# Second layer's attention: weighing by the values two key tiles in a row, and a quad's output copied out one step later

## Chip, cores and metric

One NeuronCore of one Trainium2 chip runs the whole program. The metric is the device time of one execution in microseconds. The five engines run their own instruction streams and meet at semaphores: TensorE (PE; PEld is its weight load), VectorE (DVE), ScalarE (ACT), GpSimd (POOL) and SyncE (SP), which here issues the DMAs.

## What is computed

A model of two layers over `x` (4 x 256 tokens of width 256), each layer with a cross attention to a context of 1601 keys per batch and a feed-forward part. The change touches only the second layer's attention:

```python
q = _qdq(x) @ _qdq(wq).T + bq
k, v = jnp.split(cond @ wkv.T + bkv, 2, axis=-1)
# 16 heads of 16, 256 queries, 1601 keys, 4 batches
attn = jax.nn.softmax(jnp.einsum('bnhd,bmhd->bhnm', q, k) * scale, axis=-1)
o = jnp.einsum('bhnm,bmhd->bnhd', attn, v).reshape(B, N, C)
out = _qdq(o) @ _qdq(wp).T + bp
```

After it come the residual and the second layer's feed-forward part (up, gate, down, expert).

## The kernel before

The second layer's attention is the last half of the program. It is cut into 16 quads: a quad is four heads of one batch, four quads to a batch. A quad takes 13 steps, one for each tile of 128 keys (the last has 65), named here by quad and step: q3.11 is step 11 of quad 3. A step consists of these parts:

- **Scores** (L1053): four matmuls of 256 columns, keys times queries of four heads, into PSUM banks 2 and 3 for even steps, 4 and 5 for odd ones. The operands carry three extra rows that subtract each query's maximum.
- **Exponential** (L1444): one ACTIVATE of 128x1024 on ScalarE, from those banks into one of three buffers `pr`. It waits for the scores (`sc_mm`) and for the weighing of three steps earlier (`av_mm`), which has read the buffer.
- **Weighing** (`weigh`, L1074): for each of the four heads, a matmul of 17 columns of stationary values against 256 moving columns, in float32. The trace shows it as two passes for each head, so eight matmuls. The four heads write to partitions 0, 32, 64 and 96 of bank 6, so they are in four column groups of the array and start within some 10 ns of each other. A step weighs the exponentials of the step before it. Bank 6 gathers a quad's 13 steps; then ScalarE copies it out (`out_copy`, L1431, which waits for the quad's 13th weighing), and only then may the next quad's first weighing start (`po_rdy`).
- **Maxima** (L963 on TensorE, L1633 on VectorE): the scores of the next quad are computed once more, in 32 chunks of 128 queries by 400 keys, and VectorE takes each chunk's maximum. The chunks alternate between banks 0 and 1, so TensorE may be at most two chunks ahead: chunk n waits until chunk n-2 has been reduced. At the end of the 32, VectorE makes the shift rows out of them in a chain of small operations (L1636 to L1644), TensorE turns them (`shift`, L1035, step 11) and ScalarE copies them into the queries; the next quad's scores wait for that.
- **Other work** beside it by a table (`BESIDE`): keys (L851, "k") and values (L861, "v") of the next batches, turning the output (L1083, "out", step 2 of the next quad), and the rest of the layer of the batch before. Its banks are all bank 7, taken in turns.

`schedule()` decides how many maxima chunks stand in which step (mostly two or three). Inside a step `pace` spreads them over the step's PE columns: a chunk is issued whenever the share of columns passed is ahead of the share of chunks issued.

The keys of half a batch need a long way before their maxima can start: keys on TensorE, bias on ScalarE, three splitting operations of the POOL (L628, L630, L632), three DMAs out to `kscr` and six DMAs back into the stacked layout `kst` (L545). The DMAs back overwrite a stack in use, so they also wait for the scores of two stages (a stage is two quads) earlier. `max_scores` for the first chunk of a stage waits for them (`k_stk`).

Of the kernel before, what the change touches and what calls it, by code (L numbers as in the profile page):

```python
# [28 lines left out]
B, LQ, D = 4, 256, 256  # L29
# [18 lines left out]
KT = (KEYS + P - 1) // P  # L48
# [3 lines left out]
QUADS = STAGES * 2  # L52
STEPS = QUADS * KT
# [58 lines left out]
def kind(job):  # L112

    return job[-1] if job[0] == "tail" else job[0]
# [7 lines left out]
def step_work(jobs):  # L122

    cost = {"k": 8 * 401, "v": 16 * D, "out": 2 * 4 * P, "shift": 8 * P, "up": 16 * D, "down": 16 * D,
            "expert": 16 * D, "turn_x": 4 * 4 * P, "turn_o": 4 * P, "project": 4 * D, "gate": 4 * 4 * E}
    return 4 * LQ + 4 * LQ + sum(cost.get(kind(j), 0) for j in jobs)
# [10 lines left out]
def first_chunks(t, third):  # L137

    slot = 3 * (t - TILES) + third
    return range(slot * NMAX // 6, (slot + 1) * NMAX // 6)  # L140


BESIDE = schedule()


def program(nc, x_in, ctx_in, ctx0_in, seg_in, ident_in, tabs_in, kk_in, ones_in, wkvc_in, wkr_in, wkrs_in,
# [3 lines left out]
    with ExitStack() as ctx:  # L150
# [8 lines left out]
        def bank(i, n=1):  # L159
            return ps[:, i * 512:(i + n) * 512]  # L160
# [524 lines left out]
        def _(pe):  # L685
# [169 lines left out]
            def values(b, j, bnk, between=None):  # L855
                for i in range(2 * j, min(2 * j + 2, KT)):
                    n = P if i < KT - 1 else KLAST
                    for k in range(FC):
                        if i % 2 + k >= 1 and between:
                            between(4 * D)  # L860
                        last = mm(bank(bnk)[0:n, (i % 2) * D:(i % 2 + 1) * D], ctxT[:, k, i * P:i * P + n],  # L861
                                  wkvT[:, k, D:2 * D], start=k == 0, stop=k == FC - 1)
                last.then_inc(v_mm, 1)
# [87 lines left out]
            def max_scores(quad, n):  # L951

                b, s, u, c = quad // 4, quad // 2, n // len(CH), n % len(CH)
                h = 4 * (quad % 4) + u // 2
                ca = 8 * len(CH) * quad + n
                if n == 0:
                    pe.wait_ge(k_stk[s % 2], 96 * (s // 2 + 1))
                    pe.wait_ge(q_stk[b], 96)
                if ca >= 2:
                    pe.wait_ge(mx_rdy, ca - 1)  # L960
                a, m = CH[c]
                q0 = b * LQ + (u % 2) * P
                mm(bank(ca % 2)[:, 0:m], qst[0:SROWS, h, q0:q0 + P], kst[0:SROWS, s % 2, h % HALF, a:a + m],  # L963
                   start=True, stop=True).then_inc(mx_mm, 1)
# [218 lines left out]
            shift(0)  # L1183
            pe.wait_ge(v_ev, NV + 5)
            values(1, 6, 4)
            for quad in range(QUADS + 2):
                for kt in range(KT):
                    jobs = BESIDE.get((quad, kt), [])
                    maxima = [j for j in jobs if j[0] == "max"]
                    others = [j for j in jobs if j[0] != "max"]  # L1190

                    total, count = step_work(others), len(maxima)
                    passed = [0]

                    def pace(columns):

                        passed[0] += columns
                        while maxima and (count - len(maxima)) * total < count * passed[0]:
                            max_scores(*maxima.pop(0)[1:])

                    if quad < QUADS:
                        pace(1)
                        scores(quad, kt, 0)
                        pace(2 * LQ)
                        scores(quad, kt, 2)
                        pace(2 * LQ)
                        if quad or kt:
                            weigh(KT * quad + kt - 1)
                        pace(4 * LQ)
                    elif quad == QUADS and kt == 0:  # L1210
                        weigh(STEPS - 1)
                    beside(others, pace)
                    while maxima:
                        max_scores(*maxima.pop(0)[1:])


        @block.scalar
        def _(act):
# [208 lines left out]
            def out_copy(quad):  # L1427
                act.wait_ge(av_mm, KT * (quad + 1))
                if quad >= 2:
                    act.wait_ge(ot_mm, quad - 1)  # L1430
                fn(poS[quad % 2], bank(6)[:, 0:LQ], ACT.Copy).then_inc(po_rdy, 1)  # L1431
# [4 lines left out]
            for quad in range(QUADS + 2):  # L1436
                for kt in range(KT):
                    if quad < QUADS:
                        i = KT * quad + kt
                        n = P if kt < KT - 1 else KLAST  # L1440
                        act.wait_ge(sc_mm, i + 1)
                        if i >= 3:
                            act.wait_ge(av_mm, i - 2)
                        fn(pr[i % 3][0:n, :], bank(2 + 2 * (i % 2), 2)[0:n, :], ACT.Exp, scale=SCALE1)\  # L1444
                            .then_inc(ex_rdy, 1)
                    if kt == 0 and 1 <= quad <= QUADS:
                        out_copy(quad - 1)
                    beside(quad, kt)

# [438 lines left out]
```

## Time and profile before

| what | value |
|---|---|
| median of 3 runs | 852.65 us (852.61 to 862.78) |
| span of the profiled execution | 856.0 us |
| TensorE busy | 774.2 us, 90% |
| VectorE busy | 579.5 us, 68% |
| ScalarE busy | 383.9 us, 45% |
| GpSimd busy | 187.4 us, 22% |
| first exponential of the second attention | 374.9 us |
| last exponential | 831.6 us |

The attention's 208 steps take the stretch from 374.9 to 832 us. TensorE's matmuls are pipelined, so "busy" counts a matmul of 256 columns as some 270 ns although the next one starts 110 ns later. Where a price is wanted, the starts of successive groups are to be compared, not the durations. A bracket at a row's end gives the idle time of the engine before that row and who ended it.

### The profile page before, as it was taken

The numbers are of one execution on the slowest core, as the hardware profiler recorded it, in microseconds if no ns is written. First come the engines' busy times: TensorE is split into PE (matmuls) and PEld (weight loads), VectorE is DVE, ScalarE is ACT, GpSimd is POOL, SyncE is SP. The second block draws the span as 40 slices with busy tenths as digits, with TensorE's granted clock in tenths as the row PEclk, the third lists the DMA queues.
The fourth block names the chain that finished last, engine by engine and source line by source line (L and its number), as shares of the span: only waits on it lengthen the run. The fifth ranks groups of instructions, "written<-read, shape, count | busy, mean of one in ns | idle before, by whom it ended". The sixth has DMA issues, their size and how long they took to land.

```text
span 856.0 us, 12968 instructions
## 1 busy us (share of the span) xinstructions
PE 774.2 (90%) x5027; PEld 434.2 (51%) x5027; DVE 579.5 (68%) x1290; ACT 383.9 (45%) x563; POOL 187.4 (22%) x136
## 2 busy tenths in 40 slices
PE   6998999977999898889989899989899989889996
PEld 3534777744665565644434455534445544335434
DVE  4798767621857656777867687757687757857814
ACT  2100444344333323156746565546465546544680
POOL 2377323311902122200401304002104004000000
PEclk9899999999999999999989899999799999869999
DMA  9201100004499233450381650562640750830000
GB/s 305 103 0 30 49 1 1 1 2 175 97 150 134 72 37 56 53 87 2 85 89 53 137 63 2 118 69 77 122 54 1 131 55 2 140 34 1 14 1 13
DMA packets 31708, 55.94 MB, mean 65 GB/s; under 512 B 10804, under 2 KB 19764, under 8 KB 30741
## 3 DMA queue, kind: packets, MB, share of 16 engines
q1 hardware_dynamic: 31640, 55.03, 34.2%
q8 instruction: 43, 0.70, 0.4%
q14 instruction: 25, 0.20, 0.1%
HBM read 42.56 MB, written 12.46 MB: 64 GB/s over the span
## 4 chain that ended last, share of the span: by engine, by line
PE 52%; issue 15%; DMA 12%; DVE 11%; POOL 7%; SPq 2%; ACT 2%; POOLq 0%; DVEq 0%; ACTq 0%
DMA r<-kscr 10%; PE ps L963 8%; PE ps L1074 7%; PE ps L1053 5%; PE ps L851 5%; PE ps L783 3%; PE ps L820 3%; PE ps L927 3%; PE ps L907 2%; DVE small L1633 2%; PE ps L861 2%; PE ps L810 2%; POOL r L610 2%; DMA kscr<-r 2%; PE ps L739 1%
## 5 line engine op out<-in xcount | busy, mean ns | idle before, releaser
L1633 DVE TENSOR_REDUCE small<-ps 128x1 f32<-128x400 f32 (+1 forms) x512 | 286.4, 572 | 113.8 <-PE ps L963 108.0
L1444 ACT ACTIVATE r<-ps 128x1024 f32<-128x1024 f32 (+1 forms) x208 | 212.4, 1023 | 113.2 <-PE ps L1053 110.8
L963 PE MATMUL ps<-r 96*128 96x400 bf16 (+1 forms) x512 | 176.0, 351 | 29.4 <-DMA r<-kscr 15.8
L1074 PE MATMUL ps<-r 128*17 128x256 f32 (+1 forms) x1664 | 135.4, 399 | 2.2 <-ACT r L1444 2.0
L1053 PE MATMUL ps<-r 99*128 99x256 bf16 (+1 forms) x832 | 131.5, 282 | 0.0
L963 PEld LDWEIGHTS ps<-r 96*128 96x128 bf16 x512 | 50.2, 98 | 147.0 <-DVE small L1633 95.0
L1053 PEld LDWEIGHTS ps<-r 99*128 99x128 bf16 (+1 forms) x832 | 83.8, 102 | 34.0 <-issue 11.6
L628 POOL TENSOR_TENSOR r<-r 128x1601 bf16<-128x1601 f32 x8 | 26.0, 3254 | 222.2 <-ACT r L1285 222.2
L907 PE MATMUL ps<-r,hT 128*128 128x512 f32 (+1 forms) x160 | 67.5, 554 | 1.0 <-DVE r L1622 1.0
L851 PE MATMUL ps<-r,wkvT 128*128 128x400 f32 (+1 forms) x128 | 53.4, 516 | 6.4 <-issue 6.4
L861 PE MATMUL ps<-wkvT,r 128*128 128x256 f32 (+1 forms) x208 | 58.1, 398 | 0.0
L1074 PEld LDWEIGHTS ps<-r 128*17 128x17 f32 (+1 forms) x1664 | 27.9, 96 | 54.5 <-issue 45.4
L610 POOL TENSOR_TENSOR r<-r 64x512 f32<-64x512 f32 x32 | 40.4, 1262 | 25.8 <-DVE r L1559 23.7
L618 POOL TENSOR_TENSOR r<-r,small 128x1024 f32<-128x1024 f32 x16 | 30.1, 1899 | 66.6 <-DVE small L1586 66.6
L861 PEld LDWEIGHTS ps<-wkvT,r 128*128 128x128 f32 (+1 forms) x208 | 40.1, 198 | 7.7 <-issue 1.1
L672 POOL TENSOR_TENSOR small<-small 128x2 f32<-128x2 f32 x4 | 2.8, 691 | 187.2 <-DVE small L1763 187.2
L597 POOL TENSOR_TENSOR small<-small 128x1 f32<-128x1 f32 x24 | 14.0, 583 | 118.9 <-DVE small L1470 118.9
L1329 ACT ACTIVATE r<-ps,small 128x128 f32<-128x128 f32 x64 | 19.9, 364 | 43.0 <-DVE small L1610 23.8
L1296 ACT ACTIVATE r<-ps 128x512 f32<-128x512 f32 (+1 forms) x28 | 15.9, 566 | 50.6 <-PE ps L861 50.6
L1284 ACT ACTIVATE r<-ps,bk 128x400 f32<-128x400 f32 (+1 forms) x32 | 19.1, 596 | 42.6 <-PE ps L851 42.6
L907 PEld LDWEIGHTS ps<-r,hT 128*128 128x128 f32 x160 | 28.4, 193 | 18.4 <-issue 16.3
L739 PE MATMUL ps<-r 96*128 96x512 f32 x64 | 32.2, 627 | 5.1 <-DVE r L1552 4.3
(201 smaller groups left out, 1023.7 us busy)
## 6 DMA issues: line engine op xcount, KB each, us to landing
r<-kscr SPq DMA_DIRECT2D x48, 400.2 KB, 13.6
kscr<-r SPq DMA_DIRECT2D x24, 400.2 KB, 4.0
r<-in_ctx_dram SPq DMA_DIRECT2D x4, 1601.0 KB, 7.0
r<-qscr SPq DMA_DIRECT2D x24, 128.0 KB, 5.0
r<-in_wo_dram SPq DMA_DIRECT2D x1, 2048.0 KB, 12.0
r<-in_gu_dram SPq DMA_DIRECT2D x1, 2048.0 KB, 7.8
qscr<-qpart SPq DMA_DIRECT2D x24, 64.0 KB, 1.8
x<-in_x_dram SPq DMA_DIRECT2D x1, 1024.0 KB, 5.3
```

The lines of the kernel that those rows point to most:

```text
L610: nc.gpsimd.tensor_tensor(q, q, ropet[n % 2][at, :], ALU.add).then_inc(q_rdy, 1)
L618: nc.gpsimd.tensor_tensor(sm[t % 2][:, heads, :], sm[t % 2][:, heads, :], rec0[t % 2][:, heads].unsqueeze(2).to_broadcast([P, H // 2, K0]) ...
L628: nc.gpsimd.tensor_tensor(kpart[s][1], kf[s], kpart[s][0], ALU.subtract).then_inc(ks_a, 1)
L739: mm(bank(n % 4), weff[:, h, :], qcT[:, at], start=True, stop=True).then_inc(qa_mm, 1)
L851: last = mm(bank(bnk)[:, 0:n], wkvT[:, k, (s % 2) * P:(s % 2 + 1) * P], ctxT[:, k, a:a + n], start=k == 0, stop=k == FC - 1)
L861: last = mm(bank(bnk)[0:n, (i % 2) * D:(i % 2 + 1) * D], ctxT[:, k, i * P:i * P + n], wkvT[:, k, D:2 * D], start=k == 0, stop=k == FC - 1)
L907: last = mm(bank(n % 3)[:, 0:w.shape[2]], hT[t % 2][:, k, :], w[:, k, :], start=k == 0, stop=k == FC - 1)
L963: mm(bank(ca % 2)[:, 0:m], qst[0:SROWS, h, q0:q0 + P], kst[0:SROWS, s % 2, h % HALF, a:a + m], start=True, stop=True).then_inc(mx_mm, 1)
L1053: last = mm(bank(2 + 2 * (i % 2), 2)[0:n, k * LQ:(k + 1) * LQ], kst[0:SROWS + 3, s % 2, h % HALF, kt * P:kt * P + n], qst[0:SROWS + 3, h, ...
L1074: last = mm(bank(6)[32 * k:32 * k + VW, 0:LQ], vx[0:n, b % 2, kt, h, :], pr[i % 3][0:n, k * LQ:(k + 1) * LQ], start=kt == 0, stop=kt == KT ...
L1444: fn(pr[i % 3][0:n, :], bank(2 + 2 * (i % 2), 2)[0:n, :], ACT.Exp, scale=SCALE1)\
L1633: v.tensor_reduce(mxc[quad % 2][:, n:n + 1], bank(ca % 2)[:, 0:m], AX_X, ALU.max).then_inc(mx_rdy, 1)
```

## The change

Weighing is taken out of even steps and done for two key tiles in a row in odd steps, and in step 12. Step 1 weighs the last tile of the quad before (that is one tile), step 3 tiles 0 and 1, step 5 tiles 2 and 3, and so on; step 12 weighs tiles 10 and 11. `out_copy` moves from step 0 to step 1 of the next quad, behind that step's exponential. How many maxima a step has is not changed, but `pace` counts a step's columns with the weighing that it now has. No instruction is added or removed: there are still 208 weighings and 480 chunks of maxima beside the scores.

```diff
+def closes_group(kt):
+    return kt % 2 == 1 or kt == KT - 1
+
+def previous_group(quad, kt):
+    i = KT * quad + kt
+    first = i - 1 if kt % 2 == 1 else i
+    if kt == 1:
+        return [first - 1] if quad else []
+    return [first - 2, first - 1]
...
-                    total, count = step_work(others), len(maxima)
+                total = step_work(others) + 4 * LQ * (len(weighs) - 1 if quad < QUADS else 0)
...
-                        if quad or kt:
-                            weigh(KT * quad + kt - 1)
-                        pace(4 * LQ)
-                    elif quad == QUADS and kt == 0:
-                        weigh(STEPS - 1)
+                for i in weighs:
+                    weigh(i)
+                if weighs:
+                    pace(4 * LQ * len(weighs))
...
+                    if quad == QUADS and kt == 0:
+                        step(quad, kt, [STEPS - 1])
+                    elif quad >= QUADS or not closes_group(kt):
+                        step(quad, kt, [])
+                    else:
+                        step(quad, kt, previous_group(quad, kt))
...
-                    if kt == 0 and 1 <= quad <= QUADS:
+                    if kt == (1 if quad < QUADS else 0) and 1 <= quad <= QUADS:
                         out_copy(quad - 1)
```

TensorE before, steps q1.4 and q1.5 with the first chunk of q1.6. L963 is a chunk of maxima, L1053 the scores, L1074 a weighing (four matmuls in the program); r2 and r1 hold keys and queries, r6 and r3 values and exponentials:

```order
L963 MATMUL ps<-r1,r2 128x400
L1053 MATMUL ps<-r2,r1 128x256 x4
L963 MATMUL ps<-r1,r2 128x400
L1074 MATMUL ps<-r6,r3 17x256 x4
L963 MATMUL ps<-r1,r2 128x400
L1053 MATMUL ps<-r2,r1 128x256 x4
L963 MATMUL ps<-r1,r2 128x401
L1074 MATMUL ps<-r6,r3 17x256 x4
L963 MATMUL ps<-r1,r2 128x400
```

The same place after the change, with the new line numbers: L977 is a chunk, L1067 the scores, L1088 a weighing. It begins with the last chunk of q1.3 and ends with the first of q1.6:

```order
L977 MATMUL ps<-r1,r2 128x401
L977 MATMUL ps<-r1,r2 128x400
L1067 MATMUL ps<-r2,r1 128x256 x2
L977 MATMUL ps<-r1,r2 128x400
L1067 MATMUL ps<-r2,r1 128x256 x2
L977 MATMUL ps<-r1,r2 128x400
L1067 MATMUL ps<-r2,r1 128x256 x4
L1088 MATMUL ps<-r6,r3 17x256 x8
L977 MATMUL ps<-r1,r2 128x401
L977 MATMUL ps<-r1,r2 128x400
```

The two weighings stand together (x8). The chunks, which stood at two to a step with scores or a weighing between any two, now come as a run of four with only two pairs of scores inside it, and from one run to the next TensorE has a stretch of scores and both weighings.

ScalarE before, where quad 3 ends and quad 4 begins (L1444 exponential, L1431 `out_copy`, L1296 copy of the next batch's values):

```order
L1444 ACTIVATE r<-ps 65x1024
L1444 ACTIVATE r<-ps 128x1024
L1431 ACTIVATE r<-ps 128x256
L1296 ACTIVATE r<-ps 128x32x16
L1444 ACTIVATE r<-ps 128x1024 x3
```

And after (L1468 exponential, L1455 `out_copy`, L1320 values):

```order
L1468 ACTIVATE r<-ps 65x1024
L1468 ACTIVATE r<-ps 128x1024
L1320 ACTIVATE r<-ps 128x32x16
L1468 ACTIVATE r<-ps 128x1024
L1455 ACTIVATE r<-ps 128x256
```

`out_copy` is now behind the copy of the values and behind one more exponential. The copy of the values still waits for all weighings of the batch before, the last of which TensorE now does one step later. That meeting is at the start of quads 4 and 8 only.

## Rows read from the trace of the kernel before

**Rows 1.** The page: busy tenths of TensorE and its granted clock in 40 slices

```profile
PE   6998999977999898889989899989899989889996
...
PEclk9899999999999999999989899999799999869999
```

**Rows 2.** The timeline, TensorE: plain steps of quad 1 (start us, us, instruction)

```profile
410.44 0.34 PE L963 MATMUL ps<-r 96*128 96x400 bf16 x1
410.62 0.60 PE L1053 MATMUL ps<-r 99*128 99x256 bf16 x4
411.06 0.34 PE L963 MATMUL ps<-r 96*128 96x401 bf16 x1
411.32 0.62 PE L1074 MATMUL ps<-r 128*17 128x256 f32 x8
411.88 0.34 PE L963 MATMUL ps<-r 96*128 96x400 bf16 x1
```

**Rows 3.** The timeline, TensorE: steps q4.1 and q4.2, the second without a chunk before its weighing

```profile
488.17 0.34 PE L963 MATMUL ps<-r 96*128 96x400 bf16 x1
488.35 0.60 PE L1053 MATMUL ps<-r 99*128 99x256 bf16 x4
488.88 0.63 PE L1074 MATMUL ps<-r 128*17 128x256 f32 x8
489.44 0.34 PE L963 MATMUL ps<-r 96*128 96x400 bf16 x1
489.62 0.38 PE L1083 MATMUL ps<-ident,r 128*128 128x128 f32 x2
489.84 0.33 PE L963 MATMUL ps<-r 96*128 96x401 bf16 x1
```

**Rows 4.** The timeline, TensorE and VectorE: two, then four chunks close together, quad 0

```profile
387.70 0.51 PE L963 MATMUL ps<-r 96*128 96x400 bf16 x2
388.04 0.60 PE L1053 MATMUL ps<-r 99*128 99x256 bf16 x4
388.70 0.34 PE L963 MATMUL ps<-r 96*128 96x400 bf16 x1
...
393.51 0.50 PE L963 MATMUL ps<-r 96*128 96x400 bf16 x2
393.85 0.83 PE L851 MATMUL ps<-r,wkvT 128*128 128x400 f32 x2
394.52 0.33 PE L963 MATMUL ps<-r 96*128 96x400 bf16 x1
395.08 0.33 PE L963 MATMUL ps<-r 96*128 96x401 bf16 x1 [0.23 <-DVE small L1633]
...
393.88 1.59 DVE L1633 TENSOR_REDUCE small<-ps 128x1 f32<-128x400 f32 x3 [0.27 <-PE ps L963]
```

**Rows 5.** The chain that ended last: key stacks by DMA

```profile
425.16 21.43 DMA r<-kscr
...
549.85 21.32 DMA r<-kscr
```

**Rows 6.** The timeline, TensorE: what it starts after its long idle times

```profile
446.63 0.52 PE L963 MATMUL ps<-r 96*128 96x401 bf16 x1 [4.01 <-DMA r<-kscr]
...
571.22 0.50 PE L963 MATMUL ps<-r 96*128 96x401 bf16 x1 [4.15 <-DMA r<-kscr]
...
602.94 0.27 PE L1035 MATMUL ps<-identb,nst 128*3 128x128 bf16 x1 [2.80 <-DVE nst L1644]
...
838.07 0.38 PE L1103 MATMUL ps<-identb,xq 128*128 128x128 bf16 x4 [1.58 <-DVE xq L1743]
```

**Rows 7.** The timeline, VectorE, POOL and TensorE around the shift rows of q3.11

```profile
474.46 3.06 DVE L1641 SCALAR_TENSOR_TENSOR small<-small,nst 128x8 f32<-128x8 f32 x1
...
474.24 3.26 POOL L632 TENSOR_TENSOR r<-r 128x1601 bf16<-128x1601 f32 x1
...
478.08 0.61 PE L1035 MATMUL ps<-identb,nst 128*3 128x128 bf16 x8 [2.60 <-DVE nst L1644]
```

**Rows 8.** Stretches: us, busy us of PE, PEld, DVE, ACT, POOL, clock, DMA share, GB/s

```profile
478.10:485.90 7.80, 7.80 (x43) 4.06 (x44) 3.67 (x7) 3.44 (x4) 0.00 (x0) 0.56 0.72 207
...
602.50:612.20 9.70, 9.26 (x44) 4.98 (x45) 4.09 (x9) 3.44 (x4) 0.06 (x1) 0.50 0.59 169
...
838.10:848.00 9.90, 7.60 (x43) 4.70 (x43) 3.77 (x11) 1.19 (x2) 0.69 (x1) 1.00 0.01 2
```

**Rows 9.** The timeline, TensorE in quad 15, which has no maxima beside it

```profile
821.83 0.61 PE L1053 MATMUL ps<-r 99*128 99x256 bf16 x4
822.45 0.62 PE L1074 MATMUL ps<-r 128*17 128x256 f32 x8
823.01 0.61 PE L1053 MATMUL ps<-r 99*128 99x256 bf16 x4
```

**Rows 10.** The timeline, ScalarE, q4.0 to q4.1

```profile
486.93 0.60 ACT L1296 ACTIVATE r<-ps 128x512 f32<-128x512 f32 x1 [3.32 <-PE ps L861]
487.54 1.02 ACT L1444 ACTIVATE r<-ps 128x1024 f32<-128x1024 f32 x1
```

**Rows 11.** One line's instructions: `out_copy` (durations min/median/max)

```profile
L1431 ACT ACTIVATE r<-ps x16: 376/380/393, 402.9 to 833.4; 128x256 f32<-128x256 f32 x16
```

More of the change, by code:

```diff
@@ L1185, in _, with step, pace @@
             values(1, 6, 4)
+            def step(quad, kt, weighs):
+                jobs = BESIDE.get((quad, kt), [])
+                maxima = [j for j in jobs if j[0] == "max"]
+                others = [j for j in jobs if j[0] != "max"]
+                total = step_work(others) + 4 * LQ * (len(weighs) - 1 if quad < QUADS else 0)
+                count = len(maxima)
+                passed = [0]
+                def pace(columns):
+                    passed[0] += columns
+                    while maxima and (count - len(maxima)) * total < count * passed[0]:
+                        max_scores(*maxima.pop(0)[1:])
+                if quad < QUADS:
+                    pace(1)
+                    scores(quad, kt, 0)
+                    pace(2 * LQ)
+                    scores(quad, kt, 2)
+                    pace(2 * LQ)
+                for i in weighs:
+                    weigh(i)
+                if weighs:
+                    pace(4 * LQ * len(weighs))
+                beside(others, pace)
+                while maxima:
+                    max_scores(*maxima.pop(0)[1:])
@@ L1186, in _ @@
             for quad in range(QUADS + 2):
                 for kt in range(KT):
-                    jobs = BESIDE.get((quad, kt), [])
-                    maxima = [j for j in jobs if j[0] == "max"]
-                    others = [j for j in jobs if j[0] != "max"]
-                    total, count = step_work(others), len(maxima)
[L1193 to L1206, printed above, removed]
-                        if quad or kt:
-                            weigh(KT * quad + kt - 1)
-                        pace(4 * LQ)
-                    elif quad == QUADS and kt == 0:
-                        weigh(STEPS - 1)
-                    beside(others, pace)
@@ L1213, in _ @@
-                    while maxima:
-                        max_scores(*maxima.pop(0)[1:])
+                    i = KT * quad + kt
+                    if quad == QUADS and kt == 0:
[4 more added lines that the diff above has]
+                        step(quad, kt, previous_group(quad, kt))
         @block.scalar
```

## Prediction

> **What bounds the kernel now.** I read the page first. TensorE is busy in every slice, 90% over the span, and its granted clock dips in some slices of the second half [rows 1]. The change lies in the 457 us from 374.9 us on, so I went to the timeline there. In a plain step TensorE runs without a gap: a chunk, then scores 0.18 us later, the next chunk 0.44 us after those, the weighing 0.26 us later, the next step's chunk 0.56 us later. That is 1.44 us a step, 2.88 us for two [rows 2]. So plain steps are TensorE's.
>
> Where chunks stand closer, VectorE sets the pace. Two chunks together and a third behind four scores take 1.00 us from first to third; TensorE alone would need 0.17 + 0.18 + 0.44 = 0.79. Four chunks close together take 1.57 us, and the bracket names VectorE [rows 4]. Its reductions follow each other every (1.59 - 0.57)/2 = 0.51 us, which fits: each chunk beyond the third costs another 0.5 us.
>
> Third, in some places neither binds. The key stacks come by DMA, 21.3 us from the moment a stack is free or written [rows 5], and at q2.11 and q6.11 TensorE idles 4.01 and 4.15 us for them [rows 6]; q10.11 and q12.11 show the same wait. At q3.11 and q7.11 it idles 2.60 and 2.80 us for the shift rows [rows 6, 7]: a small VectorE operation took 3.06 us, from 474.46 to 477.52, the end of a POOL operation that had begun at 474.24. What TensorE does in the steps ahead of those six points costs nothing as long as the idle time lasts.
>
> **The change, part by part.**
>
> *Fewer changes between weighing and the rest.* Four scores take 0.44 us ahead of a chunk but 0.53 us ahead of a weighing [rows 2, 3]: 0.09 us for going in. A float32 pass over 128 columns takes 0.11 us (two in 0.22, the turns at 489.62) [rows 3], so the two passes over 256 columns take 0.44 us, and the weighing's 0.56 us hold 0.12 us for coming out. Together 0.21 us for each weighing that stands alone. A quad goes from 13 groups to 7, so 6 x 16 = 96 of these go. The trace has no second weighing behind a first; I take 0.44 us for it (its passes alone), as between the columns of one weighing. The other bound is 0.65 us, when it pays in and out all the same; then this gain is nothing.
>
> The Trainium skill ("TensorEngine Tiling (Array Packing)", Key Properties) states that a change of tiling mode drains TensorE, and that a change of tile within the mode does not. By that rule alone the change is worth 96 x 0.21 = 20 us. The 0.09 and 0.12 us agree with it.
>
> *Chunks in runs.* An even step now has no weighing. Its two chunks, the last of the step before and the first of the next make a run of four. TensorE alone would pass it in 0.17 + 0.18 + 0.22 + 0.17 + 0.22 = 0.96 us; with VectorE it takes the 1.57 us of [rows 4]. Then come 0.18 + 0.53 + 0.44 + 0.56 = 1.71 us to the next run. Two steps take 3.28 us instead of 2.88, although 0.21 us is saved: a stall of 0.61 us for each plain even step. With three chunks in the even step the run has five: 2.08 us against 1.13, a stall of 0.95. An even step whose chunks stand beside keys has 0.39 (1.57 against 1.18).
>
> *Counting.* I counted these in the new order outside the stretches that end at one of the six idle points (q2.0 to 2.10, q3.6 to 3.11, q5.10 to 6.10, q7.6 to 7.11, q9.10 to 10.10, q11.6 to 12.10). These contain 30 of the 96 joinings, and 6 more are in quad 15, below. Outside:
>
> - 60 joinings, 60 x 0.21 = -12.6 us.
> - 17 runs of four, +10.4 us; 3 beside keys, +1.2 us; 4 runs of five, +3.8 us; the opening run of nine in quad 0 (1.00 + 6 x 0.51 = 4.06 against 2.76), +1.3 us.
> - Today's stalls of three close chunks, 14 x 0.21, go: -2.9 us.
> - `out_copy`, 0.38 us [rows 11]. Today the next weighing is queued behind it; after, it has until step 3, but the turn of step 2 is behind it. Normally ScalarE's exponential ends by the time the weighing of step 1 does, and `out_copy` ends as TensorE reaches the turn: nothing. At q4.0 and q8.0 the copy of the values (0.60 us) now waits for the weighing of step 1 with the exponential (1.02 us) and `out_copy` behind it [rows 10]. Weighing ends at 487.61 + 0.63 = 488.24; with 0.60 + 1.02 + 0.38 it is 490.3, and TensorE would be at the turn at 489.62 - 0.56 = 489.06 [rows 3]. That is 1.3 us, twice: +2.6 us.
> - Quad 15 has no chunks. Two steps take (823.01 - 821.83) + 1.10 = 2.28 us [rows 9], about two exponentials of 1.02 us. After, an exponential of an odd step waits for the first weighing behind its own scores: 0.53 + 0.44 + some 0.3 us to its end + 1.02 = 2.3. I take +0.4 us in all and no saving.
>
> Sum: +4.2 us. VectorE's other work and the DMA issues are not moved; no queue of SP or POOL is passed.
>
> *Hidden.* In the six stretches the same terms give +1.5 us (q2), +1.2 (q3 and q7 each), +1.8 (q6 and q10 each), +2.5 (q11 to q12). All are smaller than the idle time there, so that time shrinks instead: from 4.01 to 2.5 us at q2.11, 2.60 to 1.4 at q3.11, 2.80 to 1.6 at q7.11, 4.15 to 2.4 at q6.11. If the cover were gone, they would cost 10 us.
>
> *The clock.* After each of the idle times of 2.6 us and more stands a stretch at 1.2 GHz instead of 2.4: 478.1 to 485.9 us at a mean of 0.56, 602.5 to 612.2 at 0.50. After an idle time of 1.58 us at 838 us the clock stayed at 1.00 [rows 6, 8]. At q3.11 and q7.11 I expect 1.4 and 1.6 us. If the clock stays up there, 7.8 x 0.44 + 9.7 x 0.50 = 8.3 us come back. Against it, TensorE is less occupied in the steps before than it is today. I count half: -4.1 us. At the other points, idle for 2.2 to 2.5 us, I leave the clock as it is.
>
> **Sum**: 856.0 + 4.2 - 4.1 = 856.1 us of span. The profiled execution is 3.4 us above the median of 852.65; on that scale I forecast 853 us.
>
> **Rivals.**
>
> 1. *The joinings win.* VectorE has time on average (0.51 us a chunk, two chunks in 1.44 us), and if a run stalled less than [rows 4] say, the 17 + 4 + 1 runs would cost little. Then -12.6 - 2.9 + 2.6 + 0.4, and the clock's 8.3 on top: 856 - 21 = 835 us of span, 832 us. Against it: TensorE may be only two chunks ahead, and the 1.57 us were measured with even more TensorE work between the chunks. The rule of the skill, with nothing against it, would give 833 us, the same side.
>
> 2. *The clock falls more often.* TensorE's plain steps get some 10% less work per us. If it fell to 1.2 GHz in a part of them, a pair of steps would take about twice its TensorE time, 2 x 2.67 = 5.3 instead of 3.28 us. It would need 9 of the about 45 plain pairs to lose 17 us and be more than 2% slower: 853 + 4 + 17 = 874 us. For it: half the stretches after idle times are long. Against it: quad 0's steps today, 3.3 us a pair with five chunks, hold the full clock.
>
> 3. *A second weighing costs as much as a first.* Then the 12.6 us are gone, partly also in the hidden stretches, which still have room: 853 + 13 = 866 us.
>
> 4. *All of it is hidden.* Only 69 of the 208 steps stand ahead of an idle time, so this holds in part only; it would be 852 us, inside my forecast.
>
> **Chances.** The forecast with its half of the clock, or with all or nothing of it (849 to 857), 0.65; rival 1, in part or whole, 0.13; rival 2, 0.10; rival 3, 0.12. The range of 841 to 866 takes in the forecast, rival 3 and the part of rival 1 in which half the stalls come. A difference of 2%, 17 us, is about what can be told from no change. Faster by more, below 836 us: 0.09. Slower by more, above 870 us: 0.11. Within: 0.80.
>
> **What would show it.** In the new trace a plain pair of steps should take 3.28 us, with VectorE named in front of the chunk that opens the odd step, and a double weighing 1.00 us from its start to the next chunk. The idle time at q2.11 should be near 2.5 us, at q3.11 near 1.4 us and the clock there at 1.00. At q4.2 and q8.2 TensorE should wait 1.3 us for ScalarE. I am wrong if runs of chunks pass in under 1.3 us, if the double weighing takes 1.2 us, or if the low clock covers a different number of us than today for a reason other than q3.11 and q7.11.

## The result, and the profile after

The changed kernel is slower: 884.66 us (883.06 to 886.29, 4 runs) against 853.95 us (852.61 to 862.78, 4 runs) of the kernel before. The ratio is 1.033, with a 95% interval of 1.029 to 1.037. The forecast was 853 us, with a range up to 866; more than 870 us had a chance of 0.11. Medians of different runs are compared below as they stand, but each ratio is taken against executions of the kernel before that were measured beside it, and its interval reaches 0.25 to 0.7% to either side. A difference of medians is therefore good to a few us only.

The page of the changed kernel: two rows of the engines, the granted clock in 40 slices, and two groups of TensorE (count, then busy us and mean ns, then idle us just before them and what ended most of it).

```profile
PE 772.1 (87%) x5027; PEld 440.4 (50%) x5027; DVE 585.0 (66%) x1290; ACT 382.8 (43%) x563; POOL 187.0 (21%) x136
...
PEclk9899999999999999899999998989997989989999
...
L977 PE MATMUL ps<-r 96*128 96x400 bf16 (+1 forms) x512 | 168.6, 348 | 52.0 <-DVE small L1657 33.6
...
L865 PE MATMUL ps<-r,wkvT 128*128 128x400 f32 (+1 forms) x128 | 54.2, 522 | 10.1 <-issue 5.9
```

TensorE does the same work in the same busy time (772 us). What is new is idle time: 52.0 us ahead of the maxima, 33.6 of them ended by VectorE. The same group of the kernel before reads:

```profile
L963 PE MATMUL ps<-r 96*128 96x400 bf16 (+1 forms) x512 | 176.0, 351 | 29.4 <-DMA r<-kscr 15.8
```

The amount of low clock is not the reason: its mean is 0.956 after and 0.955 before. Where the low clock lies has changed, though, and two of the new stretches stand behind the collisions described below (528.7 to 535.6 us and 661.9 to 672.1 us).

Where the time went, from the start of each quad's first exponential to that of the next (us; profiled spans 883.2 and 856.0, first exponentials at 379.0 and 374.9):

| quad | 0 | 1 | 2 | 3 | 4 | 5 | 6 | 7 | 8 | 9 | 10 | 11 | 12 | 13 | 14 |
|---|---|---|---|---|---|---|---|---|---|---|---|---|---|---|---|
| before | 27.1 | 22.3 | 29.2 | 28.8 | 31.3 | 30.5 | 34.5 | 29.4 | 31.6 | 30.5 | 34.3 | 30.6 | 29.6 | 31.6 | 21.3 |
| after | 27.7 | 24.5 | 28.7 | 28.2 | 31.9 | **39.5** | 34.7 | 29.6 | 31.9 | **39.9** | 35.0 | 31.0 | 30.5 | 30.0 | 21.5 |

Quads 5 and 9 hold 18.4 of the 27.2 us between the two spans. The start of the first exponential holds 4.1 more; it lies in the part that the change doesn't touch, and in the profiles of the experiments it falls anywhere from 374.9 to 379.6 us. Everything else together is some 5 us. That is the difference of two single executions. In the attention alone the profile of before takes 456.7 us from the first exponential to the last, and that of e4 below, which has the same order of work, takes 445.3. So 5 us is not a measure of what the rest of the change costs; e1 below gives that.

The timeline of the changed kernel around q5.1, TensorE, VectorE and POOL (start, duration, instruction, and in brackets the idle time before it and who ended it):

```profile
520.20 0.94 PE L865 MATMUL ps<-r,wkvT 128*128 128x400 f32 x2 [0.56 <-ACT r L1309]
...
521.83 0.51 PE L977 MATMUL ps<-r 96*128 96x400 bf16 x2
...
522.20 1.06 DVE L1657 TENSOR_REDUCE small<-ps 128x1 f32<-128x400 f32 x2 [0.27 <-PE ps L977]
...
523.17 6.67 DVE L1791 TENSOR_SCALAR xn<-x,small 128x256 f32<-128x256 f32 x2
523.18 3.22 POOL L642 TENSOR_TENSOR r<-r 128x1601 bf16<-128x1601 f32 x1 [2.23 <-ACT r L1309]
...
526.48 3.21 POOL L644 TENSOR_TENSOR r<-r 128x1601 f32<-128x1601 f32 x1
529.76 1.04 DVE L1657 TENSOR_REDUCE small<-ps 128x1 f32<-128x400 f32 x2
530.38 0.52 PE L977 MATMUL ps<-r 96*128 96x400 bf16 x1 [5.53 <-DVE small L1657]
```

The same place before the change:

```profile
515.35 0.33 PE L963 MATMUL ps<-r 96*128 96x401 bf16 x1
...
516.21 0.73 DVE L1767 TENSOR_SCALAR xn<-x,small 128x256 f32<-128x256 f32 x2
...
516.70 3.32 POOL L628 TENSOR_TENSOR r<-r 128x1601 bf16<-128x1601 f32 x1 [2.24 <-ACT r L1285]
```

The two TENSOR_SCALARs normalise the tokens of the batch before (`xn`). Before, they begin 0.49 us ahead of the POOL's first splitting operation and take 0.73 us. After, they are recorded as beginning 0.01 us ahead of it and take 6.67 us, two POOL operations long. Each of the two takes 3.37 us, so the second begins at about 526.47 us, again 0.01 us ahead of a POOL operation. The maxima's reductions are queued behind them on VectorE, TensorE may be only two chunks ahead, and so it idles 5.53 us. q9.1 shows the same, 5.53 us again. Quad 5 is 9.0 us longer than before: beside the idle time, TensorE then runs at 1.2 GHz until 535.6 us.

What moved them together is `pace`. The step q5.0 has chunks and keys but, after the change, no weighing; with fewer columns counted, its last chunk falls behind all of the keys and next to the first chunk of q5.1 (521.83, x2). Two reductions in a row (1.06 us) now stand ahead of the normalisation instead of one, and the 0.49 us of lead are gone. Counted from the start of the last keys (514.67 before, 521.15 after), the POOL begins 2.03 us later in both; the normalisation began 1.54 us later and now begins 2.02 us later.

### The profile page after: what moved, and what is told of

Read it like the earlier page. It is cut to its first block, busy times and chain, and to the rows that moved or that the text cites. A ratio compares the mean times of both kernels' runs of the same rounds, so it can differ in the third digit from the quotient of the medians.

```text
span 883.2 us, 12968 instructions
## 1 busy us (share of the span) xinstructions
PE 772.1 (87%) x5027; PEld 440.4 (50%) x5027; DVE 585.0 (66%) x1290; ACT 382.8 (43%) x563; POOL 187.0 (21%) x136
## 4 chain that ended last, share of the span: by engine, by line
PE 53%; DVE 17%; DMA 12%; POOL 7%; issue 6%; ACT 3%; SPq 2%; DVEq 0%; POOLq 0%; ACTq 0%
DMA r<-kscr 10%; PE ps L1088 8%; PE ps L977 8%; PE ps L1067 5%; DVE small L1657 5%; PE ps L865 5%; PE ps L797 3%; PE ps L834 3%; PE ps L941 3%; PE ps L875 2%; POOL r L624 2%; PE ps L921 2%; PE ps L824 2%; DMA kscr<-r 2%; DVE xn L1791 1%
## 5 line engine op out<-in xcount | busy, mean ns | idle before, releaser
L1657 DVE TENSOR_REDUCE small<-ps 128x1 f32<-128x400 f32 (+1 forms) x512 | 278.4, 572 | 131.0 <-PE ps L977 127.5
L1468 ACT ACTIVATE r<-ps 128x1024 f32<-128x1024 f32 (+1 forms) x208 | 211.4, 1024 | 146.6 <-PE ps L1088 89.1
L977 PE MATMUL ps<-r 96*128 96x400 bf16 (+1 forms) x512 | 168.6, 348 | 52.0 <-DVE small L1657 33.6
L1067 PE MATMUL ps<-r 99*128 99x256 bf16 (+1 forms) x832 | 138.5, 279 | 1.6 <-ACT r L1468 1.6
L977 PEld LDWEIGHTS ps<-r 96*128 96x128 bf16 x512 | 46.8, 98 | 154.9 <-DVE small L1657 92.0
L1088 PE MATMUL ps<-r 128*17 128x256 f32 (+1 forms) x1664 | 118.1, 399 | 0.3 <-ACT r L1468 0.3
L1067 PEld LDWEIGHTS ps<-r 99*128 99x128 bf16 (+1 forms) x832 | 83.6, 102 | 38.4 <-issue 7.3
L865 PE MATMUL ps<-r,wkvT 128*128 128x400 f32 (+1 forms) x128 | 54.2, 522 | 10.1 <-issue 5.9
L1088 PEld LDWEIGHTS ps<-r 128*17 128x17 f32 (+1 forms) x1664 | 38.2, 98 | 47.2 <-issue 23.9
L624 POOL TENSOR_TENSOR r<-r 64x512 f32<-64x512 f32 x32 | 40.4, 1262 | 26.6 <-DVE r L1583 24.5
L1320 ACT ACTIVATE r<-ps 128x512 f32<-128x512 f32 (+1 forms) x28 | 15.9, 567 | 49.5 <-PE ps L875 43.9
L1609 DVE TENSOR_REDUCE small<-r 128x8 f32<-128x1024 f32 x16 | 19.1, 1194 | 26.1 <-ACT r L1291 26.0
```

Of the source, the lines that this page charges most:

```text
L624: nc.gpsimd.tensor_tensor(q, q, ropet[n % 2][at, :], ALU.add).then_inc(q_rdy, 1)
L865: last = mm(bank(bnk)[:, 0:n], wkvT[:, k, (s % 2) * P:(s % 2 + 1) * P], ctxT[:, k, a:a + n], start=k == 0, stop=k == FC - 1)
L1067: last = mm(bank(2 + 2 * (i % 2), 2)[0:n, k * LQ:(k + 1) * LQ], kst[0:SROWS + 3, s % 2, h % HALF, kt * P:kt * P + n], qst[0:SROWS + 3, h, ...
L1088: last = mm(bank(6)[32 * k:32 * k + VW, 0:LQ], vx[0:n, b % 2, kt, h, :], pr[i % 3][0:n, k * LQ:(k + 1) * LQ], start=kt == 0, stop=kt == KT ...
L1657: v.tensor_reduce(mxc[quad % 2][:, n:n + 1], bank(ca % 2)[:, 0:m], AX_X, ALU.max).then_inc(mx_rdy, 1)
```

## Experiments

### Was it the meeting with the POOL?

**e1**: the change, with the POOL's splitting held until the normalisation is done.

```diff
                 if b >= 1:
                     rsqrt3(b - 1)
+                    pool.wait_ge(n3_rdy, b)
                 if b + 1 < B:
                     split_keys(2 * b + 2)
```

> The changed kernel, with one wait added on the POOL: before the splitting of the keys of the next batch it waits until the second normalisation of the layer (n3_rdy, steps q5.1 and q9.1) is done. It delays the POOL by 1 to 2 us, in stretches that have no waits of TensorE for it. Theory A (a VectorE operation of the normalisation that starts after the POOL's has to wait until the POOL's ends; in the changed kernel it comes 0.01 us too late, and the 8.7 us from the exponential of q5.1 to the next, where 1.9 us stood before, are that): the two steps are back at 2 to 2.5 us, the span of quads 5 and 9 falls from 39.5 and 40.0 us to 30.5 to 31.5, with less of the low clock behind them, and the time falls by 16 to 19 us, to 866 to 869 us. Theory B (the stall is the chunks in runs and ScalarE's queue, out_copy behind the turn of q5.2, and the POOL has no part): the step stays at 8 us or more and the time at 884.

Measured: 868.11 us (866.26 to 874.28), ratio to the kernel before 1.017 (1.010 to 1.024). That is 16.5 us below the changed kernel by the medians, and some 14 by the ratios (1.033 and 1.017). Its timeline at q5.1:

```profile
521.07 0.72 DVE L1792 TENSOR_SCALAR xn<-x,small 128x256 f32<-128x256 f32 x2
...
521.88 3.24 POOL L642 TENSOR_TENSOR r<-r 128x1601 bf16<-128x1601 f32 x1 [3.02 <-DVE xn L1792]
...
523.71 1.54 DVE L1745 TENSOR_TENSOR r<-r,rows 128x128 f32<-128x128 f32 x1
...
525.92 0.34 PE L978 MATMUL ps<-r 96*128 96x400 bf16 x1 [0.69 <-DVE small L1658]
```

The normalisation takes 0.72 us again, the POOL's first operation stands behind it, the 5.53 us of idle time are gone, and quads 5 and 9 take 32.3 us each instead of 39.5 and 39.9. That is 14.8 us, so most of the gain lies where it was expected. The two quads were expected at 30.5 to 31.5. They stay above it in part because another VectorE operation now meets the POOL: L1745, with two inputs, takes 1.54 us where its median is 0.28, and TensorE idles 0.69 us behind it.

This run is also the change without its collision (but for the smaller meeting of L1745), and it is still 14 us slower than the kernel before. The experiments from e3 on are about those 14 us.

**e4**: the same line in the kernel before, as a control.

> Control: the kernel before with the same added wait of the POOL. By theory A the normalisation of q5.1 and q9.1 already ends before the POOL starts (516.94 against 516.70 us for its start, the second operation having started before it), so the wait changes nothing: 853 us, within 1 us. If the wait gave something of its own, this would be faster too and the first kernel's gain would prove less.

Measured: 853.74 us (848.66 to 860.6), ratio 0.998 (0.994 to 1.003). So the wait by itself gives nothing; what e1 gains is the collision's. (The expectation says that the normalisation ended before the POOL began. By its own figures it ended 0.24 us later, at 516.94 against 516.70; it had begun earlier.)

**e2**: the collision made in the kernel before, with weighings one by one. Only the last chunk of q5.0 and of q9.0 is kept until the step's end.

```diff
-                        while maxima and (count - len(maxima)) * total < count * passed[0]:
+                        while len(maxima) > ((quad, kt) in ((5, 0), (9, 0))) and \
+                                (count - len(maxima)) * total < count * passed[0]:
```

> The kernel before, where in steps q5.0 and q9.0 alone the last chunk of maxima stands behind the keys and not between their halves, as the change places it; all weighings stay single. Theory A: the keys end 0.17 us earlier, so the POOL starts 0.17 us earlier, near 516.5 us, and the normalisation comes behind two reductions in a row, near 516.6 us; it then starts behind the POOL's operation and waits 3.2 to 6.7 us, twice: 862 to 871 us. Theory B (it takes the double weighing or the moved out_copy): no difference beyond 1 us, 853 us.

Measured: 867.7 us (865.94 to 868.59), ratio 1.013 (1.007 to 1.019). That is 13.6 us above the kernel before by the medians and 11 by the ratio. Quads 5 and 9 take 38.4 and 38.0 us where they took 30.5. VectorE, POOL and TensorE at q5.1:

```profile
517.51 1.05 DVE L1634 TENSOR_REDUCE small<-ps 128x1 f32<-128x400 f32 x2 [0.94 <-PE ps L963]
518.48 6.67 DVE L1768 TENSOR_SCALAR xn<-x,small 128x256 f32<-128x256 f32 x2
518.49 3.22 POOL L628 TENSOR_TENSOR r<-r 128x1601 bf16<-128x1601 f32 x1 [2.06 <-ACT r L1286]
...
525.69 0.52 PE L963 MATMUL ps<-r 96*128 96x400 bf16 x1 [5.19 <-DVE small L1634]
```

Two chunks moved by less than a microsecond cost this kernel 11 to 14 us, with nothing else of the change in it. The place of one chunk in q5.0 and in q9.0 is enough to make the collision (e2), and the loss goes when the collision is kept from happening (e1).

### What the runs of chunks cost

**e3**: e1, and the chunks spread otherwise. A step's columns are counted without its double weighing, an even step's without any, and a step with a double weighing begins with scores instead of a chunk.

```diff
-                total = step_work(others) + 4 * LQ * (len(weighs) - 1 if quad < QUADS else 0)
+                double = len(weighs) == 2
+                total = step_work(others) - (4 * LQ if quad < QUADS and len(weighs) != 1 else 0)
...
-                    pace(1)
+                    if not double:
+                        pace(1)
...
-                if weighs:
-                    pace(4 * LQ * len(weighs))
+                if len(weighs) == 1:
+                    pace(4 * LQ)
```

> The first of these kernels, and the chunks of maxima placed anew: a step with two weighings has its chunks between its scores and before the weighings, none at its start and none behind the weighings. In a plain pair the order is chunk, 2 scores, chunk, 4 scores, chunk, 2 scores, chunk, two weighings. Theory A' (a run of four chunks stalls TensorE for 0.6 us because VectorE needs 0.51 us each, and the joining itself saves 0.21 us): the pair falls from 3.2 us to 1.02 + 0.48 + 0.26 + 1.00 = 2.75 us, below the 2.88 of before; outside the stretches hidden by the key stacks that is 20 pairs x 0.5 = 10 us under the first of these kernels, 856 us, and 845 to 856 if other steps gain too. Theory B' (the joining brings something else that costs): it stays above 862 us.

Measured: 857.73 us (854.0 to 861.94), ratio 1.004 (1.001 to 1.007): 10.4 us below e1. The timelines of TensorE through a plain pair of steps, first e1:

```profile
416.37 0.51 PE L978 MATMUL ps<-r 96*128 96x400 bf16 x2
...
417.38 0.34 PE L978 MATMUL ps<-r 96*128 96x400 bf16 x1 [0.28 <-DVE small L1658]
...
418.57 1.06 PE L1089 MATMUL ps<-r 128*17 128x256 f32 x16
419.56 0.51 PE L978 MATMUL ps<-r 96*128 96x400 bf16 x2
```

and then e3:

```profile
417.98 0.34 PE L978 MATMUL ps<-r 96*128 96x400 bf16 x1
418.16 0.38 PE L1068 MATMUL ps<-r 99*128 99x256 bf16 x2
418.38 0.33 PE L978 MATMUL ps<-r 96*128 96x400 bf16 x1
418.55 0.66 PE L1068 MATMUL ps<-r 99*128 99x256 bf16 x4
419.05 0.34 PE L978 MATMUL ps<-r 96*128 96x401 bf16 x1
419.22 0.38 PE L1068 MATMUL ps<-r 99*128 99x256 bf16 x2
419.47 0.34 PE L978 MATMUL ps<-r 96*128 96x400 bf16 x1
419.75 1.06 PE L1089 MATMUL ps<-r 128*17 128x256 f32 x16
420.74 0.34 PE L978 MATMUL ps<-r 96*128 96x400 bf16 x1
```

The pair takes 419.56 - 416.37 = 3.19 us in e1 and 420.74 - 417.98 = 2.76 us in e3, without a bracket that names VectorE; before the change it was 2.88 us [rows 2]. The count of TensorE's waits agrees: from 374 to 860 us it waits for VectorE ahead of a chunk 8 times in the kernel before, 6.4 us in all, 52 times in e1, 18.2 us, and 17 times in e3, 6.6 us. So the stall of the runs is real and can be taken away by placing the same chunks otherwise. Still the kernel is not faster than before. The expectation had 856 us, or less if other steps gained too.

**e9**: e3 without the POOL's wait. It asks if e3's other places for the chunks would have kept clear of the POOL by themselves.

> The changed kernel with the chunks spread ahead of the double weighings, and without the POOL's added wait. Theory A (the normalisation meets the POOL because the last chunk of q5.0 and q9.0 stands behind the keys; the spreading does not touch these steps, which weigh nothing): both losses of 8 us stay, 857.7 + 16 = 874 us, and steps q5.1 and q9.1 take over 8 us to the next exponential. Theory B (the collision comes from the whole kernel being late, and a faster one escapes it): 858 us.

Measured: 875.9 us (873.66 to 878.52), ratio 1.024 (1.019 to 1.030). Quads 5 and 9 take 41.0 and 41.3 us, with TensorE idle 5.31 us in each. They would not: here too the normalisation is recorded 0.01 us ahead of the POOL and is held.

```profile
520.37 6.67 DVE L1793 TENSOR_SCALAR xn<-x,small 128x256 f32<-128x256 f32 x2
520.38 3.22 POOL L642 TENSOR_TENSOR r<-r 128x1601 bf16<-128x1601 f32 x1 [1.75 <-ACT r L1311]
```

### The later `out_copy`

**e5** is e1, and **e6** is e3, with `out_copy` back in step 0:

```diff
-                    if kt == (1 if quad < QUADS else 0) and 1 <= quad <= QUADS:
+                    if kt == 0 and 1 <= quad <= QUADS:
```

> The changed kernel with the POOL's added wait (as the first experiment), and out_copy back in step 0 of the next quad on ScalarE: it waits there for the weighing of TensorE's step 1 and then goes first, ahead of the copy of the values and the exponential of step 1. Theory A (moving it behind them costs TensorE the waits of 1.18 us at the turns of q4.2 and q8.2 and 0.15 us at the others, 4.3 us in all by the trace): 2 to 4 us less than the 868.1 of the first experiment, 864 to 866. Theory B (the exponential of step 1, which is then late by up to 1 us, holds up the weighings or scores of step 3 by as much): the same time or more, 868 to 870.

Measured: 869.74 us (865.36 to 871.89), ratio 1.020 (1.017 to 1.024), beside a kernel before of 851.61 us. The waits at the turns of q4.2 and q8.2 are gone, as expected, but the time is not lower than e1's: quad 1 goes from 24.5 to 25.9 us. This is theory B of the expectation.

> The third experiment (POOL's added wait, chunks spread ahead of the double weighings) with out_copy back in step 0. Theory A: 2 to 4 us under the 857.7 of the third experiment, 854 to 856, about the time of the kernel before. Theory B: 858 to 860.

Measured: 864.3 us (859.76 to 867.17), ratio 1.013 (1.009 to 1.017), where e3 has 1.004. It is above both theories. ScalarE and TensorE at the start of quad 1:

```profile
406.38 0.38 ACT L1458 ACTIVATE r<-ps 128x256 f32<-128x256 f32 x1 [2.62 <-PE ps L1089]
...
407.61 1.95 ACT L1471 ACTIVATE r<-ps 128x1024 f32<-128x1024 f32 x2
...
408.70 0.39 PE L1068 MATMUL ps<-r 99*128 99x256 bf16 x2 [0.47 <-ACT r L1471]
```

With `out_copy` ahead of it, the exponential of step 1 waits on ScalarE for the last weighing of the quad before, which TensorE now does in step 1, behind the scores. `out_copy` ends its wait at 406.38, the exponentials come at 407.61, behind two copies of keys (L1311 and L1312), and the scores of step 3 wait for their banks. In e6 TensorE waits for an exponential ahead of scores 15 times, 5.5 us in all, against 5 times and 1.6 us in e3. So moving `out_copy` belongs to the change: without it the spread kernel loses some 7 to 8 us (e6 against e3). In e5 against e1 the loss is 1.6 us by the medians, which the intervals don't tell from nothing.

### Joining only where it is free

**e7** is e6, and **e8** is e3, with a single weighing taken early in the even steps that have keys, and in quad 15; only the plain even steps have none.

```diff
+                    early = quad < QUADS and not closes_group(kt) and \
+                        (quad == QUADS - 1 or any(j[0] == "k" for j in BESIDE.get((quad, kt), [])))
...
+                    elif not closes_group(kt):
+                        step(quad, kt, previous_group(quad, kt + 1)[:1] if early and i >= 2 else [])
+                        taken_early[0] = int(early and i >= 2)
                     else:
-                        step(quad, kt, previous_group(quad, kt))
+                        step(quad, kt, previous_group(quad, kt)[taken_early[0]:])
+                        taken_early[0] = 0
```

> The kernel of the run before this one, with the weighings joined only where nothing is lost by it: even steps that have keys beside them, and all of quad 15, weigh one tile again. Theory A (in even steps without a weighing the keys' first matmul comes 0.7 us before ScalarE has emptied bank 7, 8 times, 5.5 us by the trace of the first experiment; in quad 15 the joining costs 0.08 us a pair): 4 to 6 us less, 848 to 852, and faster than the kernel before by 2 to 6 us, since the plain pairs take 2.76 us instead of 2.88. Theory B (the wait at the keys is only passed on to the next chunk): the same as the run before, 854 to 856.

> The third experiment (POOL's added wait, chunks spread, out_copy in step 1 as the change has it), with weighings joined only where the even step has no keys, and not in quad 15. Theory A (both repairs add up: the keys no longer wait 0.6 us at bank 7, 8 times, 4.7 us by the trace of the third experiment, and quad 15 takes 13.0 us to its last exponential instead of 14.6): 5 to 7 us less than 857.7, 851 to 853, level with the kernel before or up to 3 us faster. Theory B (the waits moved only): 857 or more.

Measured: e7 857.11 us (854.51 to 861.57), ratio 1.007 (1.004 to 1.010), 7 us below e6, with quad 15 at 13.0 us instead of 14.2 before. e8 858.18 us (856.35 to 861.91), ratio 1.005 (1.003 to 1.008), the same as e3. Both were expected lower (848 to 852 and 851 to 853 us), and e8's quad 15 takes 14.1 us instead of the 13.0 expected. The trace of e8 shows that other waits took the place of the old ones. TensorE's waits ahead of keys are gone (3.3 us in e3), and those for `out_copy` have grown from 4.0 to 6.2 us; at q5.2 and q9.2 there are new ones of 1.06 us each. In quad 0 the single weighings cost time again: 27.2 us where e3 has 26.0.

### The wait under the shift rows

[rows 7] had shown the same kind of meeting already: a small VectorE operation of 3.06 us under a POOL operation. **e10** (on the kernel before) and **e11** (on e3) let the third splitting operation wait until the shift rows are made.

```diff
                 pool.wait_ge(ks_b, s + 1)
+                if s >= 3 and s % 2 == 1:
+                    pool.wait_ge(nst_rdy, 2 * s - 1)
                 nc.gpsimd.tensor_tensor(kpart[s][2], kf[s], kpart[s][1], ALU.subtract).then_inc(kpart_rdy, 1)
```

> The kernel before, all weighings single, with one wait added: the POOL starts the third splitting operation of stages 3, 5 and 7 only when VectorE has made the shift rows of the quad after next (q3.11, q7.11, q11.11). Theory A (VectorE's small operation of 3.06 us there waits for the POOL's operation, as the normalisation does in the changed kernel): the operation takes 0.2 us, TensorE's idle 2.60, 2.80 and 3.30 us fall to under 0.5, the one at q11.11 is taken back by the key stacks' DMA, and less of the low clock follows: 5 to 12 us less than before, 842 to 849 us. Theory B (the 3.06 us are something else, such as the operation's own semaphore): no change, 854 us.

> The third experiment (double weighings, chunks spread, normalisation ahead of the POOL) with the same second wait of the POOL. Theory A: its idle 2.95, 2.94 and 2.76 us at those places go too, 6 to 12 us less than 857.7: 846 to 852 us, so again some 4 us above its counterpart with single weighings. Theory B: 858 us.

Measured: e10 859.45 us (854.25 to 863.41), ratio 1.005 (1.002 to 1.009); e11 861.54 us (856.51 to 865.6), ratio 1.008 (1.005 to 1.012). The timeline of e10, first at q3.11, then at q4.11:

```profile
476.26 0.17 DVE L1643 SCALAR_TENSOR_TENSOR small<-small,nst 128x8 f32<-128x8 f32 x1
...
476.99 3.23 POOL L634 TENSOR_TENSOR r<-r 128x1601 bf16<-128x1601 f32 x1 [1.02 <-DVE nst L1646]
...
477.21 0.61 PE L1037 MATMUL ps<-identb,nst 128*3 128x128 bf16 x8
...
508.58 0.52 PE L965 MATMUL ps<-r 96*128 96x401 bf16 x1 [5.04 <-DMA r<-kscr]
```

The small operation takes 0.17 us, where [rows 7] had 3.06, and the idle time ahead of the shift is gone. The mechanism is as told. The gain is not (842 to 849 us were expected of e10, 846 to 852 of e11): the key parts leave the POOL later, the stack lands later (487.77 + 20.77 us in the chain), and TensorE idles 5.04 us for it at q4.11, 4.85 at q8.11 and 9.39 at q12.11. In e10 quad 3 goes from 28.8 to 24.8 us and quad 4 from 31.3 to 37.6 (28.9 and 29.5 in e4, the other profile with the same order). So holding the POOL takes the wait away from the shift rows and puts it on the key stacks, by way of POOL, DMA and maxima.

## Why the prediction was wrong, point by point

**The step that failed** is the last sentence of the counting: "VectorE's other work and the DMA issues are not moved; no queue of SP or POOL is passed." It holds for the order inside each engine's stream, and it is false in time. VectorE's normalisation and the POOL's splitting are on different engines, so no order list shows them passing; in the trace of before they stood 0.49 us apart. The change delays the one by one reduction, and 14 to 16.5 us are lost (e1), out of the 30.7 between the medians. The fact needed was in hand. [rows 7] showed a VectorE operation stretched to 3.06 us by the end of a POOL operation. The prediction used it only to explain today's idle time, and didn't ask which other VectorE operations stand close ahead of a POOL operation. The Trainium skill ("SBUF — State Buffer", "Who interferes with whom") states the rule in general: VectorE's `tensor_scalar` in a two-port mode, or an operation with two SBUF inputs (this one against a GpSimd operation that reads SBUF), and GpSimd hold a shared port pair exclusively, whoever is second waits for the whole instruction, and `tensor_reduce` takes no part. The trace agrees on the length of the wait (two operations of 3.37 us under POOL operations of 3.22; L1745, with two inputs in SBUF, 1.54 us) and on the reduction (a TENSOR_REDUCE at 481.29, under a POOL operation that ran from 480.88, took 0.19). On who is second it can't be used to a hundredth of a microsecond: in all three kernels with the collision the operation that was held is recorded 0.01 us ahead of the one that held it. Which mode the operations were in, no row shows. None of the rivals had this mechanism, and the rival for "slower" named the clock.

**The second step that failed** is the term "60 joinings, 60 x 0.21 = -12.6 us", together with waits put at nothing. e1 is the change without the collision. It is 14 us slower than the kernel before, where the sum had +4.2 us, and +0.1 with the clock. The paragraphs on the runs, the savings and the waits say where these 14 us lie.

**The runs of chunks.** The price was right. A plain pair was to take 3.28 us, with VectorE named ahead of the chunk. In the changed kernel most pairs with four chunks take 3.20 or 3.27 us, the first of quad 1 takes 3.46, and VectorE is named ahead of the third chunk of the run instead of at its end. In quad 1, 2.2 us were lost. The sum had 10.4 + 1.2 + 3.8 + 1.3 = 16.7 us of stalls, less 2.9 of today's, so 13.8. TensorE's waits for VectorE ahead of a chunk grew by 11.8 us (6.4 to 18.2 in e1), and spreading the chunks gives 10.4 us back (e3 against e1).

**The double weighing** was right: 419.56 - 418.57 = 0.99 us to the next chunk in e1, and 0.99 in the changed kernel too (412.52 to 413.51), predicted 1.00. Rival 3 is out.

**The savings of the joinings.** 60 x 0.21 = 12.6 us were counted. The kernels without stalls by long runs or by the collision and with `out_copy` where the change has it, e3 and e8, are still 3 to 5 us slower than the kernel before, not 12 us faster. In e3 the plain pair with four chunks gains 2.88 - 2.76 = 0.12 us rather than 0.21: four scores between chunks take 0.50 us (418.55 to 419.05) instead of 0.44, and the split four 0.47. A pair with three chunks gains 0.17 (2.71 to 2.54), and a pair with five gains nothing: 3.29 us before, 3.29 to 3.42 in e3. Quads 0 and 14 gain (26.0 for 27.1 us, 20.8 for 21.3), quad 1 stays at 22.3, and quads 5 and 9 lose 1.5 us each. In those two it is idle time: TensorE idles 2.0 us in quad 5 of e3, 0.55 before. Of it 0.64 stands behind the VectorE operation that meets the POOL (1.54 us long, as in e1), 0.32 ahead of keys, 0.49 ahead of the shift rows.

**Waits that were not priced.** In an even step without a weighing, the key matmuls reach bank 7 before ScalarE has emptied it (520.20, 0.56 us). The page has 10.1 us of idle time ahead of the key matmuls (L865), 6.4 before: 3.7 us. In e3 the new waits are about as large as the savings that were counted. Against the kernel before, from 374 to 860 us, TensorE's waits for `out_copy` grow from 0.6 to 4.0 us, those ahead of keys from nothing to 3.3, and those for VectorE ahead of chunks and shift rows from 12.0 to 15.9. All its idle time from the first exponential to the last is 31.4 us before and 42.7 in e3.

**`out_copy` and the values.** 1.3 us was expected at q4.2 and q8.2, and 1.18 was measured at each. The prediction's own figures give 488.24 + 0.60 + 1.02 + 0.38 - 489.06 = 1.18 too; the 1.3 is a slip. At the other turns `out_copy` costs some 1 us more in all, which was put at nothing. ScalarE's three instructions stand as worked out:

```profile
491.83 0.60 ACT L1320 ACTIVATE r<-ps 128x512 f32<-128x512 f32 x1 [2.66 <-PE ps L1088]
...
492.32 1.02 ACT L1468 ACTIVATE r<-ps 128x1024 f32<-128x1024 f32 x1
493.23 0.39 ACT L1455 ACTIVATE r<-ps 128x256 f32<-128x256 f32 x1
...
493.76 0.41 PE L1097 MATMUL ps<-ident,r 128*128 128x128 f32 x2 [1.18 <-ACT r L1455]
```

**Quad 15** went from 14.2 to 14.6 us; +0.4 was predicted.

**The hidden stretches** were right in kind and half right in size: the idle time shrank instead of the steps costing more. At q2.11 4.01 us became 2.80 (predicted 2.5), at q3.11 2.60 became 2.01 (1.4), at q7.11 2.80 became 2.49 (1.6), at q6.11 4.15 became 3.51 (2.4). At q12.11 it grew, from 3.7 to 5.46. The waits for the key stacks also differ between executions of the same order: e4 has 3.52 us at q2.11, 3.20 at q6.11 and only 0.40 at q12.11. The timeline at q3.11, with the meeting of [rows 7] in it, now 2.63 us long:

```profile
480.88 3.23 POOL L646 TENSOR_TENSOR r<-r 128x1601 bf16<-128x1601 f32 x1
...
481.52 2.63 DVE L1664 TENSOR_SCALAR nst<-small 128x8 bf16<-128x8 f32 x1
...
484.92 0.61 PE L1049 MATMUL ps<-identb,nst 128*3 128x128 bf16 x8 [2.01 <-DVE nst L1668]
```

**The clock.** The term of -4.1 us can't be counted on. The granted clock of three stretches of the changed kernel (columns as in [rows 8]), behind the shift of q3.11, behind that of q7.11, and behind the first collision:

```profile
484.90:488.30 3.40, 3.38 (x37) 2.16 (x38) 2.17 (x5) 2.19 (x3) 0.00 (x0) 1.00 0.93 362
619.30:629.00 9.70, 9.30 (x66) 5.23 (x66) 6.26 (x12) 4.22 (x5) 0.00 (x0) 0.82 0.75 190
529.70:535.40 5.70, 5.02 (x29) 2.38 (x30) 4.31 (x10) 1.50 (x2) 3.22 (x1) 0.50 0.00 0
```

At q3.11 the clock stayed at 2.4 GHz after 2.01 us of idle time, as hoped. But the collisions bring new stretches at 1.2 GHz, and in e1 the same 2.01 us at the same place was followed by 480.9 to 486.0 us at a mean of 0.67. Past 370 us the low clock holds 52.6 us in the profile of before, 54.6 after, 30.7 in e1, 44.6 in e3 and 37.2 in e4, though e4 does the work of the kernel before in the same order. Rival 2 did not come: the plain steps hold 1.00.

**What is left of the difference.** Of 30.7 us between the medians, e1 accounts for 16.5 and e3 for 10.4 more (by the ratios 14 and 11). The 3.8 that remain are e3's distance to the kernel before: the waits at the turns, beside the keys and for VectorE, and the 0.4 of quad 15, against the gain of the plain pairs. How these share the 3.8 us is added up from traces and was not tested one by one. No version was faster than the kernel before.

## What to carry to other kernels

Before costing a reordering at nothing for the engines that it doesn't touch, look in the trace for pairs of VectorE and GpSimd operations that start close to each other: which one is first, and by how much. A lead of half a microsecond is a margin that the change may eat. The price here was the length of the two GpSimd operations that followed, and everything queued behind VectorE paid it. Where work is spread by a running count of columns, taking something out of a step also moves everything that the count places, so read the new positions of the pieces at the steps with special work, not only at the plain ones. And before multiplying a saving by the number of places, sort the places by what else stands in them: the same joining gave 0.12 us with four chunks beside it and nothing with five.

## What the runs showed of the hardware

- Two VectorE operations of 0.73 us took 6.67 us when they began within 0.01 us of a GpSimd TENSOR_TENSOR of 128x1601, in the changed kernel, in e2 and in e9. Each took 3.37 us, about the length of the GpSimd operation beside it (3.22). The next GpSimd operation began only 0.08 us behind the first; one VectorE operation got through between the two, and the second was held by the next. In e9 the row of the second stands apart: 3.37 us from 523.67, with the GpSimd operation at 523.68. With a lead of 0.49 us they took 0.73, and the GpSimd operation 3.32 instead of 3.22.
- A GpSimd wait for the VectorE operation costs nothing in the kernel before (e4) and keeps this pair apart. It moves the GpSimd work, so it can meet another: in e1 and e3 a TENSOR_TENSOR of 128x128 with two inputs took 1.54 us instead of 0.28.
- A tiny VectorE operation (128x8, 0.17 or 0.18 us) is held as a large one is: single ones took 2.63 and 3.06 us.
- After equal idle times of 2.01 us at the same place the granted clock once stayed at 1.00 and once fell (0.67 over the next 5 us). Here the length of the gap alone doesn't decide it.
